# Two interleaved LSTM recurrences: the gate products in another order on TensorE, and the new state multiplied on GpSimd instead of VectorE

## What is computed

```
def _lstm(x, Wih, Whh, b):
    xW = jnp.einsum('bsd,gd->sbg', x, Wih) + b
    h0 = jnp.zeros((x.shape[0], Whh.shape[1]), x.dtype)
    def step(carry, xt):
        h, c = carry
        gates = xt + h @ Whh.T
        i, f, g, o = jnp.split(gates, 4, axis=-1)
        c = jax.nn.sigmoid(f) * c + jax.nn.sigmoid(i) * jnp.tanh(g)
        h = jax.nn.sigmoid(o) * jnp.tanh(c)
        return ((h, c), h)
    _, hs = jax.lax.scan(step, (h0, h0), xW)
```

## Time and profile before

| what | value |
|---|---|
| runs | 2376.21, 2377.60, 2378.54 us (median 2377.6) |
| span of the profiled execution, first to last instruction | 2376.3 us |
| the loop over the 224 steps, within it | 70.2 to 423.2 us, 353.0 us |
| TensorE busy over the span (matmul / weight load) | 86% / 62% |
| VectorE, ScalarE, GpSimd busy over the span | 57%, 37%, 21% |
| granted TensorE clock, mean of the span | 0.857 |

### The profile page before, as it was taken

The page is one execution under the profiler, slowest core; times in us unless marked ns, Lnnn a source line. Parts: engine busy times, 40 slices in busy tenths (PEclk is TensorE's granted clock), DMA queues, the critical chain, the costliest instruction groups (busy, mean ns, idle before and its releaser), DMA issues.

```text
span 2376.3 us, 57229 instructions
## 1 busy us (share of the span) xinstructions
PE 2041.1 (86%) x22720; PEld 1482.7 (62%) x22720; DVE 1355.0 (57%) x3605; ACT 884.5 (37%) x3421; POOL 502.1 (21%) x1131
## 2 busy tenths in 40 slices
PE   7999999998978799897977887999999998889843
PEld 3788888786656566466865654666554544556522
DVE  5666666674345688544634723787263210678797
ACT  2344444353236566211324522665111111246511
POOL 3344444221001100101324512332000000401111
PEclk9655555799988899998998998999899999789956
DMA  3000000104000000300021000000030000000000
GB/s 133 4 5 4 5 4 5 74 2 177 1 1 1 14 11 5 133 1 23 1 80 47 2 1 10 8 8 5 1 147 0 1 0 1 1 14 15 2 0 16
DMA packets 7752, 57.20 MB, mean 24 GB/s; under 512 B 760, under 2 KB 5216, under 8 KB 5728
## 3 DMA queue, kind: packets, MB, share of 16 engines
q1 hardware_dynamic: 7488, 53.54, 5.9%
HBM read 52.62 MB, written 0.92 MB: 23 GB/s over the span
## 4 chain that ended last, share of the span: by engine, by line
PE 66%; DVE 16%; issue 9%; ACT 5%; POOL 4%; DMA 1%; DVEq 0%; POOLq 0%; ACTq 0%; SPq 0%
PE banks L259 42%; PE banks L264 8%; PE banks L1323 6%; PE banks L908 3%; DVE memory L1421 2%; PE banks L934 2%; ACT memory L1352 1%; PE banks L1474 1%; ACT memory L1359 1%; DVE memory L795 1%; DVE memory L1218 1%; DVE memory L1427 1%; DVE memory L1430 1%; DVE memory L1439 1%; DVE memory L994 1%
## 5 line engine op out<-in xcount | busy, mean ns | idle before, releaser
L259 PE MATMUL banks<-memory 128*112 128x256 f32 (+7 forms) x4192 | 1130.1, 426 | 68.9 <-POOL memory L2030 8.0
L259 PEld LDWEIGHTS banks<-memory 128*128 128x128 f32 (+3 forms) x4192 | 706.7, 196 | 396.3 <-issue 250.6
L264 PE MATMUL banks<-memory 112*125 112x112 f32 (+3 forms) x2000 | 309.8, 288 | 151.0 <-DVE memory L795 92.0
L264 PEld LDWEIGHTS banks<-memory 112*125 112x125 f32 (+3 forms) x2000 | 240.3, 173 | 270.0 <-issue 139.4
L1323 PE MATMUL banks<-memory 128*128 128x8 bf16 (+2 forms) x10752 | 325.8, 175 | 25.9 <-DVE memory L1439 5.8
L1323 PEld LDWEIGHTS banks<-memory 128*128 128x128 bf16 x10752 | 304.0, 104 | 48.3 <-DVE memory L1439 46.2
L956 ACT ACTIVATE memory<-banks,memory 112x375 f32<-112x375 f32 x384 | 215.4, 579 | 26.2 <-DVE memory L994 26.0
L994 DVE TENSOR_REDUCE memory<-banks 112x2 f32<-112x750 f32 x192 | 171.1, 934 | 45.4 <-PE banks L908 43.7
L1002 DVE COPY memory<-banks 125x448 f32<-125x448 f32 x192 | 116.6, 619 | 12.8 <-PE banks L264 8.7
L1421 DVE TENSOR_REDUCE memory<-banks 128x48 f32<-128x192 f32 x448 | 109.6, 286 | 5.5 <-PE banks L1323 5.5
L1502 ACT ACTIVATE memory<-memory 112x112 f32<-112x112 f32 x192 | 71.7, 375 | 86.2 <-DVE memory L1523 86.2
(11 more groups left out here) (233 smaller groups left out, 2404.1 us busy)
## 6 DMA issues: line engine op xcount, KB each, us to landing
memory<-in_l2x SPq DMA_DIRECT2D x1, 7680.0 KB, 21.5
memory<-in_l2f SPq DMA_DIRECT2D x1, 7168.0 KB, 19.6
memory<-in_l1f SPq DMA_DIRECT2D x1, 4617.0 KB, 15.9
memory<-in_ctxT SPq DMA_DIRECT2D x24, 187.5 KB
memory<-in_l0a SPq DMA_DIRECT2D x1, 4224.0 KB, 16.1
memory<-in_l2f SPq DMA_DIRECT2D x1, 4096.0 KB, 12.9
memory<-in_l3f SPq DMA_DIRECT2D x1, 3073.0 KB, 22.4
memory<-in_l2a SPq DMA_DIRECT2D x1, 3072.0 KB, 19.2
```

Of the source, the lines that this page charges most:

```text
L259: ins = self.nc.tensor.matmul(out, weights[i], acts[i], start=i == 0, stop=i == n - 1)
L264: return self.nc.tensor.transpose(out, in_, self.ident[0:n, 0:n])
```

## The change

TensorE now issues all three weight parts of blocks 0 to 5 first, 36 matmuls, counts `gates_full` up, and then issues all three parts of blocks 6 and 7, 12 matmuls, and counts it up again. The waits for `h_hi`, `h_mid` and `h_parts` stand ahead of the weight parts of blocks 0 to 5. VectorE no longer computes the state; its new function `dve_output` adds one to tanh(o/2) into a tile `o1`, after the tanh of o, and from the second position on after an `h_hi` that says that GpSimd has read the `o1` of the position before. GpSimd multiplies `o1` by the tanh of the cell, ahead of its three other operations.

```diff
-        self.tc = wk.take(2, KD * B)
+        self.tc, self.o1 = wk.take(2, KD * B), wk.take(2, KD * B)
@@ pe
-                    for g in range(GT):
-                        for j in range(KD):
-                            own, first = (self.slots[l][0], 0) if g < 6 else (self.slots[l][1], 6)
-                            at = (g - first) * B
-                            ins = self.nc.tensor.matmul(
-                                own[:, part:3, at:at + B], whh[:, part, l, j, g * P:(g + 1) * P],
-                                self.upper[l][:, 0:3 - part, j * B:(j + 1) * B], start=part == 2 and g == first and j == 0,
-                                stop=j == KD - 1 and part == 0, skip_group_check=True)
-                        if part == 0 and g == 5:
-                            ins.then_inc(*s.gates_full.up())
+                    ins = self.pe_gates(l, part, 0, 6)
                 ins.then_inc(*s.gates_full.up())
+                for part in (2, 1, 0):
+                    ins = self.pe_gates(l, part, 6, GT)
+                ins.then_inc(*s.gates_full.up())
+
+    def pe_gates(self, l, part, first, end):
+
+        own = self.slots[l][first > 0]
+        for g in range(first, end):
+            for j in range(KD):
+                at = (g - first) * B
+                ins = self.nc.tensor.matmul(
+                    own[:, part:3, at:at + B], self.whh[:, part, l, j, g * P:(g + 1) * P],
+                    self.upper[l][:, 0:3 - part, j * B:(j + 1) * B], start=part == 2 and g == first and j == 0,
+                    stop=j == KD - 1 and part == 0, skip_group_check=True)
+        return ins
@@ pool
                 h, upper = self.h[:, l], self.upper[l]
+                G.wait_ge(*s.o_ready(2 * t + l + 1))
+                G.wait_ge(*s.tc_ready(2 * t + l + 1))
+                G.tensor_tensor(h[:, 0], self.o1[:, l], self.tc[:, l], ALU.mult).then_inc(*s.h_hi.up())
                 G.wait_ge(*s.h_hi(2 * t + l + 2))
                 G.tensor_tensor(h[:, 1], h[:, 0], upper[:, 0], ALU.subtract).then_inc(*s.h_mid.up())
@@ dve
-    def dve_state(self, t, l):
+    def dve_output(self, t, l):
         s, V = self.s, self.nc.vector
         V.wait_ge(*s.act_tanh(2 * (2 * t + l) + 2))
-        V.wait_ge(*s.tc_ready(2 * t + l + 1))
         if t:
-            V.wait_ge(*s.h_kept(2 * t + l - 1))
-        V.scalar_tensor_tensor(out=self.h[:, l, 0], in0=self.gates[:, l, 4], scalar=1.0, in1=self.tc[:, l], op0=ALU.add,
-                               op1=ALU.mult).then_inc(*s.h_hi.up())
+            V.wait_ge(*s.h_hi(2 * t + l))
+        V.tensor_scalar(self.o1[:, l], self.gates[:, l, 4], 1.0, None, ALU.add).then_inc(*s.o_ready.up())
```

More of the change, by code:

```diff
@@ L1409, in dve @@
             self.dve_cells(t, 0)
-            self.dve_state(t, 0)
+            self.dve_output(t, 0)
             self.dve_gates(t, 1, 0, 6)
@@ L1413, in dve @@
             self.dve_cells(t, 1)
-            self.dve_state(t, 1)
+            self.dve_output(t, 1)
     def dve_gates(self, t, l, first, end):
```

## The result

| | before | after |
|---|---|---|
| median of the runs | 2377.4 us (7 runs) | 2366.5 us (7 runs) |
| lowest to highest | 2376.2 to 2378.7 | 2358.1 to 2370.7 |
| span of the profiled execution | 2376.3 | 2361.4 |
| the loop, first matmul to last store | 353.0 | 336.7 |
| one round, median | 3.094 | 2.983 |

The ratio of the times is 0.9948, with a 95% interval of 0.9936 to 0.9959: the changed kernel is faster by 0.5%. The forecast was 2361.5 in a range of 2355 to 2370. In this document a median of a round, of a step or of a distance is taken over the 224 steps of a trace, without the first twenty.

The account below looks back on a forecast made before the run. The prediction took one LSTM's latency chain, 3.09 us a round, as the bound. Rounds 12.9 us less, stalls 4.0 less, GpSimd's stalls 0.8 more: 16.1 off the 2376.3 span, plus 1.3 to the median, gives 2361.5 us, range 2355 to 2370.

Parts of the forecast that it names:

- The bound: Loop of 224 steps: bound by one LSTM's latency chain, 3.09 us a round, 112 times, not by an engine's work.
- Blocks f, i, g first: TensorE's order: the reduction is released by matmul 36 instead of 44, 0.21 us earlier a round.
- The cover of the middle part: TensorE's load of `part` 1: h's middle part is ready at 0.30 us, needed at 0.32, so it fits by 0.02.
- State on GpSimd: From the start of the cell's tanh to TensorE: 0.63 us instead of 0.53, a loss of 0.10 a round.
- The stalls: VectorE's instruction supply stalls every sixteenth step; the change moves this before the second reduction and hides it, 4.0 us less.
- GpSimd's stalls: GpSimd's longer list in the loop may stall every 25.6 steps, nine times, adding 0.8 us.
- The sum: Whole loop: 12.9 us less from rounds, 4.0 less from stalls, 0.8 more from GpSimd, together 16.1 us less.
- The rule against the change: VectorE and GpSimd SBUF instructions exclude each other whole, says the skill; the prediction read 0 to 0.03 us a meeting.
- rival 3: GpSimd and VectorE collide in the loop, excluding each other for whole operations: 0.18 us a round lost, 2381 us; chance 0.05.
- Rival 2: The stall in the loop stays, or comes back on GpSimd: 4 us more, 2365.5 us; chance 0.17.
- Rival 4: Reordering gains nothing net: middle part late, TensorE stalling at `part` 1, or GpSimd's multiplication slow: 2377 us; chance 0.06.
- Rival 5: TensorE's clock rises in the loop as its share of the round grows: 6.7 us less, 2355 us; chance 0.04.

Follow-up runs that it names:

- e2_order_only: Kernel before with only the new matmul order, blocks f, i, g first; state stays on VectorE: 2377.4 us, ratio 0.9981, loop 347.9 us.
- e5_tc_first: Changed kernel with GpSimd's two waits swapped, so the multiplication itself carries the wait for the cell's tanh: 2363.0 us, ratio 0.9929, loop 331.1 us.
- e4_before_shift: Kernel before with six more VectorE instructions ahead of the loop (clearing of `gates` cut in seven): 2375.6 us, ratio 0.9981, loop 349.2 us.
- e8_after_unshift: Changed kernel with two more VectorE instructions ahead of the loop (clearing of `gates` cut in three): 2363.4 us, ratio 0.9937, loop 337.0 us.
- e1_again: Changed kernel run again, unedited: 2362.9 us, ratio to the kernel before 0.9919, loop 336.8 us.
- e3_state_only: Kernel before with only the state moved to GpSimd, matmuls in the old order: 2392.3 us, ratio 1.0044, loop 363.6 us.
- e6_order_vtc: Kernel before with blocks f, i, g first and VectorE's state instruction itself carrying the wait for the cell's tanh: 2358.6 us, ratio 0.9920, loop 330.7 us.

## Why the prediction was right, point by point

**The bound.** That the loop is the chain of one LSTM and not an engine's work was right. The clock, read as 0.50 throughout, was at its higher level for the first 2.5 us of the loop, which changes nothing in the sum. And each link that the change did not touch kept its length to 0.001 us.

**Blocks f, i, g first.** Foretold 0.21 a round; the median distance from the first matmul to the reduction fell from 1.457 to 1.241, 0.216. But this gain is there only because VectorE's list no longer holds the reduction back. The prediction said of that order that it "gives nothing by itself", which is true of the kernel before; it did not say that without the freed list the 0.21 would shrink to 0.05, as e2_order_only showed.

**The cover of the middle part.** Foretold to hold by 0.02; it held in every step: the first matmul of `part` 1 and of `part` 0 followed the one ahead of it by 0.027 us as all others do.

**State on GpSimd.** Foretold 0.63 from the tanh of the cell to TensorE, a loss of 0.10. Measured 0.362 + 0.278 = 0.640 against 0.304 + 0.232 = 0.536: a loss of 0.104. The multiplication took the assumed 0.22 us. 0.064 of the 0.640 was the additional wait, which the exchange of two lines in e5_tc_first took away.

**The stalls.** Foretold 4.0 us less from VectorE; measured 14 of 0.30, 4.2. The place was right too: the two reductions took 0.68 to 0.70 with a stall, and 0.68 was foretold. e4_before_shift shows that this shift by itself hides the stalls. What the prediction did not see is that they were hidden twice over: in e8_after_unshift the stall is back ahead of the first reduction and costs nothing either, since no wait for the tanh of the cell stands ahead of it in VectorE's list any more. The third way that the runs showed, a state that carries its late wait itself, does not apply to the changed kernel.

GpSimd's stalls, foretold as 0.8 us, were there and smaller: one in step 9 (0.345 late) and one 640 instructions later in step 137 (0.29 late), about 0.6 us in all. The second one, where the multiplication starts 0.65 behind the start of the tanh of the cell instead of 0.36:

```profile
278.71 0.22 POOL L1390 TENSOR_TENSOR memory<-memory 128x16 f32<-128x16 f32 x1 [0.86 <-ACT memory L1365]
```

**The sum.** 112 x 0.111 + 4.2 - 0.6 = 16.0 us by the measured terms, 16.1 foretold, 16.3 in the loop. The program's median fell by 11.0 in the first set of runs and by 16.4 in e1_again, for a loop that agrees to 0.1. The 5 us by which 2366.5 lies above the forecast are therefore not from the loop. In the two profiled executions the later start of the loop (1.1 us) is a part of it; the rest was not traced to a place.

**The rule against the change.** The prediction weighed two stretches in which GpSimd and VectorE run together, from nothing to 0.03 us a meeting. The changed kernel bears it out: at 201.65 the second cell operation and the store start within 0.01 of each other, and it is the store that takes 0.31 instead of 0.27. The rule of the Trainium skill (SBUF — State Buffer, "Who interferes with whom"), an exclusive lock for a whole instruction, would have kept one of them back by 0.17 us or more; the trace disagrees, for tiles this small. What rival 3 lacked was not contention but its size: it is real, up to 0.045 us, and in e3_state_only and e6_order_vtc it stands on the path.

**The rivals.** Rival 2, a stall that stays or comes back on GpSimd, is refuted by the distances of the first reductions and by the 0.6 us of GpSimd's. Rival 3 is refuted in its size. Rival 4, a late middle part or a slow multiplication, is refuted by the 0.027 and the 0.22 above; e2_order_only comes near to its time by another way, VectorE's list. Rival 5: after the first 2 to 4 us the clock stayed at 0.50 in the loop of every kernel, also at a round of 2.867.

## What to carry to other kernels

When an instruction waits for several things, let it carry the one that comes last and put the others ahead of it: here that is worth 0.06 us each time on either engine, costs nothing, and on VectorE it took 14 stalls off the path as well. Before two engines' lists are judged one edit at a time, ask which of two chains (the data's, or the order of one engine's list) becomes the longer one: two edits that are worth -5 and +11 us alone can be worth -16 together. Then ask whether both are needed: here the edit that looked like half of the gain could be replaced by two exchanged lines. And when the medians of a program scatter by some us, compare the loop in the trace, which here repeated to 0.1 us in one pair and 0.8 us in the other.

## What the runs showed of the hardware

- **The additional wait.** From the start of the tanh of the cell to an operation that waits for it: on VectorE 0.304 with the wait ahead of the instruction and 0.248 with the wait in it; on GpSimd 0.362 and 0.298.
- **A stall at every 128th instruction of VectorE.** The wait instruction at that place starts no sooner than 0.43 us behind the end of the wait instruction two places ahead (13 traces, 14 cases in each). It costs 0.28 to 0.34 us where that earlier wait has just held the engine, and nothing where the time is covered. A packet of 8192 bytes on an instruction queue follows each of them. GpSimd's visible stalls were 640 = 5 x 128 instructions apart. The Trainium skill (Runtime: NRT & Kernel Launch, "Instruction fetch mechanics") calls the cost of crossing a boundary between blocks of instructions mostly hidden, and has blocks of 256. The traces agree with "mostly" only as far as other work covers it: exposed it came to 4.2 us of 353. Their distance is 128 on VectorE, not 256.
- **Two engines that start together.** Over all thirteen traces, the first cell operation (128x32, two inputs from SBUF, 0.192 alone) took about 0.237 when GpSimd's store started in the same 0.01 us (124 cases), 0.225 when it had started about 0.02 before (700), 0.202 at 0.04 (322), and 0.192 from 0.06 on (over 900), although the store itself lasts 0.27. Where GpSimd's operation was the one that started 0.02 to 0.06 later, it was the longer one and VectorE's was not. It is as if only about the first 0.05 us of an operation were shared; which part of it that is, no run here tells apart.
